# x's groups 0 to 2 loaded ahead of the first taps, w's chunks 1 and 2 and the tables behind the last convolution operand, all remainders of gate and up on GpSimd

## The reference, cut to what matters

```
K = 2 * einsum('hn,hnl->hl', Cs, exp(dtA * l)).real        # 32 heads, 512 taps
u_m = u * (arange(512) < length)
x = x + (causal_conv(u_m, K) + u_m * D) * mask              # layer 0
gate = x @ W_gate.T + LoRA;  up = x @ W_up.T + LoRA         # 512 -> 1376
x = x + (silu(gate) * up) @ W_down.T + LoRA                 # layer 1
```

## Time and profile before

| quantity | before |
|---|---|
| time, median of 3 | 532.68 us (531.34 to 533.72) |
| the profiled execution: time / span | 533.11 us / 531.4 us |
| mean granted TensorE clock | 0.997 |
| PE busy | 494.7 us (93%) |
| DVE busy | 292.3 us (55%) |
| ACT busy | 198.0 us (37%) |
| POOL busy | 46.4 us (9%) |

### The profile page before, as it was taken

The page is one execution under the profiler, slowest core; times in us unless marked ns, Lnnn a source line. Parts: engine busy times, 40 slices in busy tenths (PEclk is TensorE's granted clock), DMA queues, the critical chain, the costliest instruction groups (busy, mean ns, idle before and its releaser), DMA issues.

```text
span 531.4 us, 9990 instructions
## 1 busy us (share of the span) xinstructions
PE 494.7 (93%) x2940; PEld 449.0 (84%) x2940; DVE 292.3 (55%) x617; ACT 198.0 (37%) x411; POOL 46.4 (9%) x55
## 2 busy tenths in 40 slices
PE   0098799999999999999999999999999999999997
PEld 0087787989898999999999999898989898989986
DVE  7883176846454555546464547373737474545541
ACT  5791006433333334334342333243434243434330
POOL 1006600100000001000000101010101010101000
PEclk9999899999999999999999999999999999999999
DMA  7899995556555656555555656464646465555520
GB/s 288 267 346 376 331 340 128 122 111 154 116 152 115 144 128 147 126 137 118 142 123 138 130 129 139 108 157 109 157 88 174 101 161 114 153 117 148 110 63 21
DMA packets 175443, 82.74 MB, mean 156 GB/s; under 512 B 128034, under 2 KB 157282, under 8 KB 175426
## 3 DMA queue, kind: packets, MB, share of 16 engines
q1 hardware_dynamic: 175426, 82.54, 60.5%
HBM read 63.46 MB, written 19.04 MB: 155 GB/s over the span
## 4 chain that ended last, share of the span: by engine, by line
PE 88%; DMA 5%; DVE 5%; issue 1%; SPq 0%; ACT 0%; DVEq 0%
PE ps_g L1111 23%; PE ps_u L1111 22%; PE ps_db L1072 13%; PE ps_da L1072 13%; PE ps_x L1064 3%; PE ps_g L1038 3%; DMA toep<-kpad 2%; DMA kpad<-k_sb 2%; PE ps_g L1121 2%; PE ps_u L1122 2%; PE ps_g L1122 2%; PE ps_u L1121 2%; PE ps_u L1038 2%; PE ps_da L1178 1%; PE ps_db L1179 1%
## 5 line engine op out<-in xcount | busy, mean ns | idle before, releaser
L1111 PE MATMUL ps_g<-w_hi,x_hi 128*128 128x512 f32 (+1 forms) x192 | 72.7, 379 | 1.4 <-DVE x_lo L995 1.4
L529 ACT CAST b_spl<-b_raw 64x512 fp32r<-64x512 f32 (+1 forms) x96 | 51.7, 571 | 55.3 <-PE ps_u L1122 35.7
L1111 PE MATMUL ps_u<-w_lo,x_hi 128*128 128x512 f32 (+1 forms) x192 | 71.4, 372 | 0.0
L1111 PE MATMUL ps_u<-w_hi,x_lo 128*128 128x512 f32 (+1 forms) x192 | 71.4, 372 | 0.0
L1111 PE MATMUL ps_g<-w_hi,x_lo 128*128 128x512 f32 (+1 forms) x192 | 71.4, 372 | 0.0
L1111 PE MATMUL ps_u<-w_hi,x_hi 128*128 128x512 f32 (+1 forms) x192 | 71.4, 372 | 0.0
L1111 PE MATMUL ps_g<-w_lo,x_hi 128*128 128x512 f32 (+1 forms) x192 | 70.9, 369 | 0.0
L876 DVE TENSOR_TENSOR b_spl<-b_raw,b_spl 64x512 fp32r<-64x512 f32 (+1 forms) x96 | 57.9, 629 | 15.3 <-ACT b_spl L529 13.7
L933 DVE TENSOR_TENSOR h_act<-h_act,ps_u 128x512 f32<-128x512 f32 (+1 forms) x48 | 30.4, 632 | 58.6 <-PE ps_u L1122 38.9
L1072 PE MATMUL ps_da<-wd_hi,ht_hi 128*128 128x288 f32 (+1 forms) x176 | 52.1, 296 | 0.0
L1072 PE MATMUL ps_da<-wd_lo,ht_hi 128*128 128x288 f32 (+1 forms) x176 | 51.9, 295 | 0.0
(11 more groups left out here) (170 smaller groups left out, 887.7 us busy)
## 6 DMA issues: line engine op xcount, KB each, us to landing
a_raw<-atab SPq DMA_DIRECT2D x64, 152.0 KB, 2.3
toep<-kpad SPq DMA_DIRECT2D x16, 512.0 KB, 7.3
b_raw<-btab SPq DMA_DIRECT2D x128, 64.0 KB, 2.1
h_raw<-hrow SPq DMA_DIRECT2D x30, 256.0 KB, 2.9
um<-xr SPq DMA_DIRECT2D x16, 256.0 KB, 5.4
x<-xT SPq DMA_DIRECT2D x8, 512.0 KB, 6.9
w_raw<-wgu SPq DMA_DIRECT2D x8, 512.0 KB, 9.1
xrow<-x_sq SPq DMA_DIRECT2D x64, 64.0 KB, 2.2
```

The costliest lines, as they stand in the source:

```text
L529: nc.scalar.copy(b_spl[b_rows(slot), up, 0:w], b_raw[b_rows(slot), up * w:(up + 1) * w]).then_inc(b_hi, 1)
L1111: T.matmul(ps[:, 0:w], xs[:, kb, :], ws[:, kb, col:col + w], start=(kb == 0 and xs is x_hi and ws is w_hi), stop=False)
```

## The change

SyncE issues x's groups 1 and 2 in place of w's chunk 1 ahead of the first taps, group 3's two halves among the first four Toeplitz loads, and the tables, chunks 1 and 2 and then `wd` after the last Toeplitz load. ScalarE makes the tops of chunk 1 after the first two b parts and before `x_hi`, those of chunk 2 after `x_hi`, and the first two of `wd` after `t_hi`. GpSimd makes all twelve remainders of w; VectorE's first two of `wd` move behind `t_lo`. TensorE's waits count accordingly.

```diff
-        NP_POOL = 2 * KB
+        NP_POOL = NP_GU
@@ sync
-            for n in range(2 * KB):
+            for n in range(KB):
                 load_piece(n)
+            for g in range(1, NG - 1):
+                for half in range(2):
+                    load_x(g, half)
...
-            load_piece(2 * KB)
             for pair in range(RC):
                 load_toep(pair, pair, 0)
-            for n in range(2 * KB + 1, NP_GU):
-                load_piece(n)
-            load_x(1, 0)
+                if pair < 2:
+                    load_x(NG - 1, pair)
             store_taps(1)
-            load_x(1, 1)
-            load_x(2, 0)
...
-            for n in range(NP_GU, len(pieces)):
+            load_a(0, 0, ids0)
+            sp.wait_ge(mask_done, KB + 1)
+            load_b(0, 0, 0, ids0)
+            for n in range(KB, len(pieces)):
                 load_piece(n)
@@ scalar
-            for n in range(4, NP_GU):
-                top_part(n)
...
             b_hi_part(0, 0, 0, 1)
+            for n in range(KB, 2 * KB):
+                top_part(n)
...
+            for n in range(2 * KB, NP_GU):
+                top_part(n)
             tiles(act, body)
@@ vector
-                if pair >= PAIRS - 6:
-                    rem_part(NP_POOL + pair - (PAIRS - 6))
@@ tensor
-                        pe.wait_ge(w_rem_pool if c < 2 else w_rem_dve, (KB, 2 * KB, KB)[c])
+                        pe.wait_ge(w_rem_pool, (c + 1) * KB)
```

More of the change, by code:

```diff
@@ L306, in _ @@
                 load_toep(pair, pair - RC, 1)
-                if pair == RC:
-                    load_x(2, 1)
                 if pair >= RC + 2:
                     store_taps(pair - RC)
-                    load_x(3, pair - RC - 2)
             def load_b(a, q, c, ids):
@@ L558, in body @@
                 na, nq = (a, 1) if q == 0 else (a + 1, 0)
-                if first:
-                    top_part(NP_GU)
-                    top_part(NP_GU + 1)
                 act.wait_ge(tm_ok, t + 1)
@@ L567, in body @@
                     nc.scalar.copy(t_hi[LR:P, up, :], src).then_inc(thi_ok, 1)
-                if not first:
+                if first:
+                    top_part(NP_GU)
+                    top_part(NP_GU + 1)
+                else:
                     ht_hi_part(t - 1, 2)
@@ L910, in body @@
                 na, nq = (a, 1) if q == 0 else (a + 1, 0)
-                if first:
-                    rem_part(NP_GU)
-                    rem_part(NP_GU + 1)
                 dve.wait_ge(a_ps, t + 1)
@@ L924, in body @@
                                         ALU.subtract).then_inc(tlo_ok, 1)
-                if not first:
+                if first:
+                    rem_part(NP_GU)
+                    rem_part(NP_GU + 1)
+                else:
                     ht_lo_part(t - 1, 2)
@@ L1159, in body @@
                 if first:
-                    pe.wait_ge(w_rem_dve, KB + 2)
+                    pe.wait_ge(w_rem_dve, 2)
                 pe.wait_ge(ad_lo, t + 1)
```

## The result

The changed kernel takes 537.7 us (median of 4, 536.85 to 538.56) where the kernel before, run beside it, takes 532.9. The ratio is 1.0093 with a 95% interval of 1.0073 to 1.0113: slower, by 4.8 us or 0.9%. The forecast was 536.2. The profiled execution of the changed kernel took 537.43 us, with a span of 535.6 and a mean granted clock of 0.986; before's took 533.11, span 531.4, clock 0.997. On these two executions the difference is 4.3 us.

The account below looks back on a forecast made before the run. It took TensorE's matmuls to bound the sixteen tiles, and loads to stand in the early stage. Layer 1's later start, +1.1 us, and the clock, +2.4, made +3.5 on 532.7, so 536.2 us; range 531.5 to 539.0.

Parts of the forecast that it names:

- Part 1: Early loads and convolutions: x first, chunks 1 and 2 later; last convolution ends at 70.1, 8.9 us earlier, without waits.
- C: Rival at the convolutions: they become bound by loads after all, at 298 GB/s; +4.8 us, 537.5; chance 0.12.
- D: Rival at the Toeplitz loads: the taps' stores, not the bytes, set when they go out; about 539; chance 0.05.
- Part 2: Between last convolution and layer 1: chunk 1's fourth piece lands at 74.0, `x_hi` starts at 75.05, only 2.4 us earlier.
- landing, by the median of 4.7, at 65.6: Last Toeplitz load, issued at 60.9: lands 4.7 us later, with the tables and chunk 1 queued behind it.
- Part 3: First tile's `x_lo` and copy on VectorE: held by GpSimd's subtractions; layer 1 starts at 81.45, 1.1 us later.
- rows of 404.56 and 98.15: Earlier trace's GpSimd copies beside VectorE subtractions: whichever came second waited, 0.47 and 1.05 us; basis for the hold.
- Rival A: At `x_lo`'s second part: VectorE is not held; -0.3 us, 532.4, or 533.7 if only the copy goes free; chance 0.20.
- Part 4: Start of layer 1: TensorE's idle time from 70.1 to 81.45 lowers its clock, costing 2.4 us, bounds 0 and 2.54.
- Rival B: TensorE's clock is kept over the idle time before layer 1; +1.1 us, 533.8; chance 0.08.
- Part 5: Rest of first tile: first silu slips about 1.3 us, but its transpose fits by 0.4; nothing added, up to 1 us otherwise.
- The sum: Start of layer 1 +1.1 and clock +2.4 give +3.5 us, so the median goes from 532.7 to 536.2.

Follow-up runs that it names:

- E1: The changed kernel, but GpSimd starts chunk 1's subtractions only when the first tile's `x_lo` is whole; 540.42 us.
- E3: The changed kernel with 52 matmuls of unused results on TensorE behind the last convolution, to keep it busy; 538.01 us.
- E4: The changed kernel with `x_hi` on ScalarE ahead of b and chunk 1's tops, and VectorE's `b_lo` parts moved later, behind `square_x`; 536.30 us.
- E7: The changed kernel with the subtractions of chunks 1 and 2 on VectorE instead of GpSimd, loads and tops unchanged; 535.36 us.
- E8: E7 with 36 matmuls of unused results on TensorE behind the last convolution; 535.94 us.
- E5: The changed kernel with the tables a and b issued early, at the ninth and tenth pair as before the change; 536.06 us.
- E6: The changed kernel with `x_hi` and `x_lo` first, chunks 1 and 2 subtracted on VectorE, and loads in order of need; 529.98 us, ratio 0.9958 to before.

## Why the prediction was right, step by step

**Part 1, the convolutions: right.** The first at 26.49 (26.6 forecast), the fifth at 41.13 (41.2), no wait after it, the end at 70.14 (82.90 - 12.76; forecast 70.1). The forecast put nothing on group 3's two loads, which now stand among the first four Toeplitz loads, and nothing was lost by them: from 26.49 on the chain stays on TensorE. Rivals C and D are out: the loads kept up at 311 GB/s (42 to 60 us) and 347 (60 to 66).

**Part 2, the landing of chunk 1: mechanism right, size 1.6 us short.** The forecast had the fourth piece at 74.0 and `x_hi` at 75.05; they came at 75.65 (67.26 + 8.39) and 76.63. The term that was mis-sized is "landing, by the median of 4.7, at 65.6": it took 6.0 us, to 67.0. How much of this is chance can be read from the other runs. E1, E3, E4, E7 and E8 issue the same loads in the same order up to there, and their last Toeplitz load landed 5.6, 5.3, 5.5, 4.7 and 5.4 us after its issue. `x_hi` started at 76.03 (E1), 75.81 (E3), 75.03 (E7) and 75.95 (E8). So 4.7 is the low end of six traces, and the changed kernel's own profile the high end; what sets it in one execution no run shows. Another 0.6 us went to the tables, for which I had 2.8 us at 379 and 229 GB/s; the three microseconds from 67 to 70 moved 166, 291 and 287. Some 0.4 came back, since the pieces followed each other by 1.27 us (406 GB/s) instead of 1.4.

**Part 3, the hold: right, its parts not.** 3.8 us were forecast and 3.8 measured, but the forecast had nothing on the first part of `x_lo`, 2.05 on the copy and 1.8 on the second part, and 0.32, 1.84 and 1.64 came. That the sums agree so closely is partly luck: each wait depends on where in GpSimd's operation VectorE asks, and E3 and E5, with the same order of work there, show 4.1 and 3.65. The forecast also calls its rows of 404.56 and 98.15 a meeting of two operations with two SBUF operands each; GpSimd's was a copy, which has one. That two-input operations on both engines hold each other is shown by the runs, not by those rows. E1 and E7 take the hold away, and with it 3.8 us between `x_hi` and the start. Rival A is out. Start of layer 1: +2.53 instead of +1.1, which is the 1.58 us of part 2 less 0.13 between `x_hi` and the start.

**Part 4, the clock: there, 1.8 us instead of 2.4.** The forecast went by the length of the idle time, and that step failed: "nearer to the longer idle time" took 2.4 of the first convolution's 2.54. The cost does not follow the length. In before's trace the fall that cost 1.88 us followed a wait of 2.08:

```profile
60.26 4.29 PE L1038 MATMUL ps_g<-um,toep 128*128 128x256 f32 x16 [2.08 <-DMA toep<-kpad]
```

Idle times of 12.76, 8.88, 8.61 and 7.71 us cost 1.82 (changed kernel), 1.49 (E5, twelve matmuls in 4.53), 1.99 (E1, in 5.03) and 2.10 (E7, in 5.14), and 9.53 us in E4 cost 2.7. Rival B is out. E3 and E8 show that the clock stays up when TensorE is kept busy, and that taking it back gives less than it costs once something else is late.

**Part 5, the rest of the first tile: right.** The first silu starts at 93.61, 10.71 us after the start; 7.65 + 1.82 of clock leaves a slip of 1.24, forecast 1.3. The first transpose follows the start by 12.54, before by 10.71: the clock again, and nothing for the slip.

**The sum.** +1.1 and +2.4 were forecast, +2.53 and +1.82 measured: +3.5 against +4.35. The two errors have opposite signs, so the sum came nearer than its terms: that is luck. What I had not seen is that the hold would be there wherever GpSimd's subtractions are put between 73 and 89 us: E1 moves it and pays more.

## What to carry to other kernels

A reordering of loads that frees the early stage moves the wait to the first consumer of what was put back: ask when the moved bytes land, and what stands behind their first use on each engine. A long row of two-input GpSimd operations held VectorE's short subtractions with two SBUF inputs and its copy from SBUF to SBUF, each by up to 1.9 us, where a GpSimd subtraction takes 1.7 to 2.4, and neither the masked copy out of PSUM nor the transpose. So a chain of small ones on the critical path can cost several times its length; taking the hold off one of them is worth nothing if the next lies on the same stretch. Put the operand that the next stage starts with ahead of the ones that it needs later, on every engine that has both in its program; in E4, where the hold was still there, that alone gave 1.0 us at the second tile.

## What the runs showed of the hardware that was not expected

- Behind the same loads the same Toeplitz load landed between 4.7 and 6.0 us after its issue in six traces.
- Four `t_lo` subtractions of 0.3 us took 6.93 and 7.00 us beside GpSimd's (1.24 alone): each of the last three takes 1.64 to 1.66 us in E1, where GpSimd's 704-wide subtractions take 1.72 on average, so they are let in one for one, not as a group.
- The microseconds with the 16-partition b table and the a table in flight moved 166 to 291 GB/s with the DMA engines busy all the time; the pieces of w alone moved 406.
- The clock fell after a wait of 5.85 us (E1, for the second time) and of 9.53 us (E4) in the middle of layer 1, and after 7.71 us in E7; it did not after 2.41 us in E6, though it did after 2.08 us in the kernel before and 1.77 us in E5. The length of the last wait alone does not tell. In E7 the twelve matmuls ran at 0.50 throughout.
